# Softmax denominators of a local attention: the reciprocal of a 1x512 row, taken instead as 128x4 after a turn through TensorE

## The chip, the cores and the metric

One Trainium2 chip, all 8 NeuronCores, one launch. Each core works alone on its own half of a sequence (no collectives). The time is that of the slowest core in device microseconds (us). Engines: PE is TensorE (PEld its weight loads), DVE is VectorE, ACT is ScalarE, POOL is GpSimd, SP is SyncE.

## What is computed

Input x of 4 sequences x 8192 tokens x 1024 channels. A linear attention layer with residual and layer norm comes first, then two layers of this kind, and a last layer norm. The part that the change touches is `local_attention`:

```python
WINDOW, HEADS, DIM_HEAD = 512, 8, 64
def local_attention(q, k, v):            # (b, 8, n, 64)
    w = n // WINDOW
    bq = q.reshape(b, h, w, WINDOW, d) * QK_SCALE
    bk, bv = look_around(k), look_around(v)      # a window and the one before it
    sim = einsum('bhwid,bhwjd->bhwij', bq, bk)
    mask = (i < j) | (i > j + WINDOW) | (j == -1)
    attn = softmax(where(mask, -max, sim), axis=-1)
    return einsum('bhwij,bhwjd->bhwid', attn, bv)
def _layer(x, ...):
    h = shift_token(x); q, k, v = split(h @ wqkv)
    q, k = rotary_xpos(l2norm(q) * qs, l2norm(k) * ksc)
    x = x + local_attention(q, k, v) @ wo
    ...                                   # then x + a gated MLP (1024 -> 2 x 2730 -> 1024)
```

## The kernel before

The activations X stay in SBUF, transposed (channels on partitions, 5248 token columns: 4096 of the core and a halo of 1152). The program is a list of operations per engine; `Sched` turns each stated dependency into a wait on a counting semaphore of the engine that does the work, and every engine executes its list strictly in the order in which the Python code adds to it. So the order of the code is the order of the queues.

For each of the two layers, the loop of `build_layer`, `for w in range(n_iter)`, runs over windows of 512 tokens. One pass projects V (`piece_v`), Q and K (`piece_q`, `piece_k`) of window w, turns Q and K to channel-major with float32 transposes on PE into the PSUM bank P[4] (`piece_T`, lines 1049 and 1063), multiplies an earlier window by `wo` (line 1115), and then does the attention of window w-1 for its 8 heads. In the part for one head the keys of that window come in four tiles of 128 (j = 0 to 3). For each tile PE computes scores of up to 640 queries into PSUM (line 1209) and adds the masks as matmuls (lines 1216, 1220), ACT takes the exponential into `pt` (lines 1223, 1227), and PE multiplies by V (`emit_pv`, lines 1164 and 1171). V has a 65th column of ones, so that row 64 of the result is the sum of the exponentials, the denominator of the softmax. Queries of the same window go to bank P[6], those of the next to P[7]; P[7] is carried in `O_acc` until the next window adds its part.

After the fourth tile comes the division, for 80 heads of the first layer and 72 of the second, 152 in all. DVE adds P[6] and `O_acc` into `tsum` (65x512, line 1242); row 64, which lies on one partition, is held above 1e-30 (line 1244), inverted (RECIPROCAL, line 1246) and cast to bf16 as `rrowb` (line 1248). PE spreads it over 64 partitions by a matmul with a column of ones (line 1250, into P[2]), and DVE multiplies (`o_sb`, line 1254). Then DVE copies P[7] to `O_acc` (line 1259); in the last window of a layer, where nothing is carried, a memset stands there. The matmul of line 1250 stands in PE's queue between the last V product of one head and the first scores of the next, so nothing of the next head starts on PE before `rrowb` is there:

```python
trp = s.add("tensor", lambda t: t.matmul(
    P[2][0:64, 0:512], sb["ones_row"][0:1, 0:64], rrowb[0:1, :],
    start=True, stop=True), [tcb, t_tt1, t_uq, t_uk])
```

Behind the two layers stands the last layer norm. Its lines 1650 to 1666 are read below for the price of operations: a RECIPROCAL of a 1x128 row (line 1650), two float32 matmuls that spread a 1x128 row over 128 partitions (lines 1655, 1658), and DVE's use of the first (line 1662).

Of the kernel before, what the change touches and what calls it, by code (L numbers as in the profile page):

```python
# [6 lines left out]
F32 = mybir.dt.float32  # L7
BF16 = mybir.dt.bfloat16
AF = mybir.ActivationFunctionType
ALU = mybir.AluOpType  # L10
# [180 lines left out]
def make_core_inputs(inputs, core):  # L191
    b, h = core // 2, core % 2
    s = 4096 * h
# [94 lines left out]
    for hh in range(8):  # L288
        hs[hh, hh, :] = 1.0
    d["hsel"] = hs  # L290
    d["halo01"] = np.full((128, 1), 1.0 if s > 0 else 0.0, np.float32)
    return d

# [5 lines left out]
class KB:  # L299
# [24 lines left out]
    def build_io(self):  # L324
        d = self.din
# [24 lines left out]
        d("tab", (TEXT, 4, DF))  # L350
        d("ones2row", (2, MEGA))
        d("halo01", (128, 1))
        d("hsel", (8, 8, 128))
        for m in ("mq_lo", "mq_hi", "mk_lo", "mk_hi", "ident", "negI"):
            d(m, (128, 128))
# [14 lines left out]
    def build_consts(self):  # L370
        s, sb, inp = self.s, self.sb, self.inp
        for n, shp, dt in [
            ("ones_row", (1, 640), BF16), ("ones_col", (128, 1), BF16),
            ("identF", (128, 128), F32),
            ("negI", (128, 128), BF16),
            ("mk_lo", (128, 128), BF16), ("mk_hi", (128, 128), BF16),
            ("eps", (128, 1), F32), ("maskrow", (128, NT_EXT), F32),
            ("zrow", (1, 512), BF16),
            ("X", (128, NCH, TEXT), BF16),
            ("lg_col0", (128, NCH), BF16), ("lb_col0", (128, NCH), BF16),  # L380
            ("lg_col1", (128, NCH), BF16), ("lb_col1", (128, NCH), BF16),
            ("b2_col0", (128, NCH), F32), ("b2_col1", (128, NCH), F32),
            ("halo01", (128, 1), F32),
        ]:
            sb[n] = self.sbuf(n + "_g", shp, dt)

        dco = s.new_dma_sem("consts", group=True)
# [3 lines left out]
        s.dma(g, sb["identF"][:, :], inp["ident"][:, :], dco)  # L391
        s.dma(g, sb["maskrow"][:, :], inp["maskrow_col"][:, :], dco)
        s.dma(g, sb["halo01"][:, :], inp["halo01"][:, :], dco)
        for l in range(2):
            s.dma(g, sb[f"lg_col{l}"][:, :], inp[f"lg_col{l}"][:, :], dco)
            s.dma(g, sb[f"lb_col{l}"][:, :], inp[f"lb_col{l}"][:, :], dco)
            s.dma(g, sb[f"b2_col{l}"][:, :], inp[f"b2_col{l}"][:, :], dco)
# [420 lines left out]
    def build_layer(self, l, do_mlp=True):  # L818
# [11 lines left out]
        with ExitStack() as es:  # L830
# [13 lines left out]
            o_sb = [self.sbuf(f"osb{l}_0", (128, 4, 512), BF16, es)]  # L844
            tsum = self.sbuf(f"tsum{l}", (65, 512), F32, es)
            rrowb = self.sbuf(f"rrowb{l}", (1, 512), BF16, es)
            ubuf = self.sbuf(f"ubuf{l}", (128, 512), BF16, es)
            qhat = self.sbuf(f"qhat{l}", (128, 512), BF16, es)
            qrot = self.sbuf(f"qrot{l}", (128, 512), F32, es)
# [51 lines left out]
            self.t_ttk = None  # L901
            self.t_qe_prev = None
            self.t_ke_prev = None
            t_pv = None
            t_oacc = None
            t_tt1 = None
# [172 lines left out]
            for w in range(n_iter):  # L1079
# [61 lines left out]
                if 0 <= pb < n_proj and (do_left or do_right):  # L1141
# [8 lines left out]
                    for h in range(HEADS_F):  # L1150
# [90 lines left out]
                        if do_left:  # L1241
                            tt1 = s.add("vector", lambda v, h=h: v.tensor_add(
                                tsum[:, :], P[6][0:65, :], O_acc[:, h, :]), [t_pv, t_oacc])
                            tmx = s.add("vector", lambda v: v.tensor_scalar(  # L1244
                                tsum[64:65, :], tsum[64:65, :], 1e-30, None, ALU.max), [tt1])
                            trc = s.add("vector", lambda v: v.reciprocal(  # L1246
                                tsum[64:65, :], tsum[64:65, :]), [tmx])
                            tcb = s.add("vector", lambda v: v.tensor_copy(  # L1248
                                rrowb[0:1, :], tsum[64:65, :]), [trc])
                            trp = s.add("tensor", lambda t: t.matmul(  # L1250
                                P[2][0:64, 0:512], sb["ones_row"][0:1, 0:64], rrowb[0:1, :],
                                start=True, stop=True), [tcb, t_tt1, t_uq, t_uk])
                            t_rep = trp
                            to2 = s.add("vector", lambda v, h=h, B=B_left: v.tensor_tensor(
                                o_sb[0][64 * (h % 2):64 * (h % 2) + 64, h // 2, :],
# [472 lines left out]
```

How the kernel before makes its waits and increments, by code:

```python
                def body(eng):  # L101
# [1 line left out]
                    for op in ops[e]:  # L103
                        for d in op.deps:
                            if d.value is None:
                                raise RuntimeError(f"unmarked dep on {e} #{op.idx}")
                            if d.dma_sem is not None:
                                key, sem = d.dma_sem, d.dma_sem.sem
                                val = d.dma_sem.count if d.dma_sem.group else d.value
                            else:
                                key, sem, val = d.engine, sems[d.engine], d.value
                            if val > seen.get(key, 0):
                                eng.wait_ge(sem, val)
                                seen[key] = val
                        inst = op.fn(eng)
                        try:
                            self.inst_map[inst.ins.name] = (e, op.idx, getattr(op, 'label', None))
                        except Exception:
                            pass
                        if op.dma_sem is not None:
                            inst.then_inc(op.dma_sem.sem, 16)
                        elif op.marked:
                            inst.then_inc(sems[e], 1)
                    return None
# [1549 lines left out]
            def fin(sy):  # L1674
                sy.wait_ge(dout[0].sem, dout[0].count)
                sy.wait_ge(dout[1].sem, dout[1].count)
                return None
# [32 lines left out]
            def fin(sy):  # L1710
                sy.wait_ge(dsem.sem, dsem.count)
                return None
```

## Time and profile before

| | |
|---|---|
| median of 2 runs | 11750.34 us (11729.5 to 11771.19) |
| profiled execution, its own time | 11762.71 us |
| its span on the slowest core (core 5) | 11761.1 us |
| spans of the eight cores | 11641.0 to 11761.1 us |
| busy in the span: PE, DVE, ACT | 6636.5 us (56%), 3399.7 us (29%), 1649.8 us (14%) |
| TensorE's granted clock, mean over the span | 0.73 of full speed |

The span runs from the first to the last instruction of a core; the execution's own time is 1.6 us longer. Records of PE overlap, since matmuls are pipelined: the length of one record is not what it costs in a row of them; the distance of two starts is. The bracket behind an instruction is how long its engine had been idle before it, and what ended that.

### The profile page before, as it was taken

Reading aid. Unit: us, or ns where it says so; the run is one execution under the profiler, and the core shown is the slowest. Engines: PE = TensorE matmul, PEld = TensorE weight load, DVE = VectorE, ACT = ScalarE, POOL = GpSimd, SP = SyncE. Lnnn points to the kernel's source line nnn. Section 1 sums busy time; section 2 is a strip of 40 time slices with the busy share of each in tenths; the row PEclk is TensorE's granted clock in tenths of the full one; section 3 lists DMA queues with packets and bytes.
Section 4 is the critical chain, followed back from the end, with each engine's and each line's share of the span. In section 5 each row is a group of like instructions: output and inputs, shape, how many; then the busy total and the mean of one; then the engine's idle time right before and its main releaser. Section 6 shows DMA issues by size and latency. Waiting matters only on the chain.

```text
span 11761.1 us, 75679 instructions; the slowest of 8 cores (11641.0 to 11761.1 us)
## 1 busy us (share of the span) xinstructions
PE 6636.5 (56%) x27498; PEld 2698.4 (23%) x27498; DVE 3399.7 (29%) x4612; ACT 1649.8 (14%) x2817; POOL 91.3 (1%) x136
## 2 busy tenths in 40 slices
PE   0488645544444445447687775544454457778731
PEld 0133212211212222213232222222122123223211
DVE  0011133333443443441112211344434421221234
ACT  0000011111212222210001000222222200000100
POOL 1000000000000000000000000000000000000000
PEclk9977777676666566656799997566666567899965
DMA  9401200001000000001122223000000001222221
GB/s 118 53 0 14 38 0 7 8 7 24 2 1 2 1 1 2 0 8 24 50 67 52 63 69 79 2 2 1 1 2 1 0 17 24 61 63 75 53 60 50
DMA packets 610314, 325.45 MB, mean 28 GB/s; under 512 B 489180, under 2 KB 541004, under 8 KB 608416
## 3 DMA queue, kind: packets, MB, share of 16 engines
q0 software_dynamic: 65024, 79.23, 5.5%
q1 hardware_dynamic: 310496, 137.55, 4.5%
q10 hardware_dynamic: 234432, 103.83, 3.5%
q8 instruction: 228, 3.74, 0.1%
q14 instruction: 134, 1.10, 0.0%
HBM read 374.31 MB, written 59.77 MB: 37 GB/s over the span
## 4 chain that ended last, share of the span: by engine, by line
PE 47%; DVE 26%; DMA 10%; issue 7%; ACT 6%; another core or an unknown queue 4%; DVEq 1%; ACTq 0%; POOL 0%; SPq 0%; POOLq 0%
PE M0b L1519 6%; PE M1b L1519 5%; DVE tsum L1246 4%; DMA w2b<-w2bf 4%; DMA w1g<-w1bf 4%; PE kps L486 3%; PE vps L497 3%; PE M0b L1576 2%; PE p2b L747 2%; PE p2b L653 2%; PE M1b L1576 2%; PE p2b L632 1%; PE L0b L1115 1%; DMA x1t<-x1b 1%
## 5 line engine op out<-in xcount | busy, mean ns | idle before, releaser
L1246 DVE RECIPROCAL tsum<-tsum 1x512 f32<-1x512 f32 x152 | 508.3, 3344 | 16.0 <-DVE tsum L1244 0.5
L1576 PE MATMUL M0b<-hbuf,w2b 128*128 128x512 bf16 (+1 forms) x1760 | 407.2, 385 | 172.0 <-DMA w2b<-w2bf 121.2
L1519 PE MATMUL M0b<-xt,w1a 128*128 128x512 bf16 (+1 forms) x1760 | 448.3, 404 | 89.2 <-DVE xt L1478 69.1
L486 PE MATMUL kps<-WkSb,X_g 128*128 128x512 bf16 x656 | 210.4, 479 | 421.1 <-DMA WvSb<-Wv 421.1
L1519 PE MATMUL M0b<-xt,w1g 128*128 128x512 bf16 (+1 forms) x1760 | 409.9, 378 | 58.6 <-DMA w1g<-w1bf 56.6
L1519 PE MATMUL M1b<-xt,w1a 128*128 128x512 bf16 x1408 | 389.7, 427 | 77.0 <-DVE xt L1478 56.7
L1552 DVE SCALAR_TENSOR_TENSOR hbuf<-M0b,gout 128x512 bf16<-128x512 f32 x220 | 143.4, 652 | 997.2 <-ACT gout L1544 985.7
L1576 PE MATMUL M1b<-hbuf,w2b 128*128 128x512 bf16 x1408 | 338.2, 391 | 131.0 <-DMA w2b<-w2bf 89.9
L1552 DVE SCALAR_TENSOR_TENSOR hbuf<-M1b,gout 128x512 bf16<-128x512 f32 x176 | 121.8, 692 | 840.9 <-ACT gout L1544 831.4
L1519 PE MATMUL M1b<-xt,w1g 128*128 128x512 bf16 x1408 | 343.7, 388 | 26.8 <-DMA w1g<-w1bf 25.3
L1223 ACT ACTIVATE pt<-L0b,mrowH 128x512 bf16<-128x512 f32 (+1 forms) x320 | 213.7, 671 | 681.7 <-PE L0b L1220 583.1
L1223 ACT ACTIVATE pt<-L1b,mrowH 128x512 bf16<-128x512 f32 (+1 forms) x320 | 213.7, 671 | 634.4 <-PE L1b L1220 536.4
L1250 PE MATMUL L0b<-rrowb,ones_row_g 1*64 1x512 bf16 x80 | 48.1, 601 | 440.6 <-DVE rrowb L1248 440.6
L1544 ACT ACTIVATE gout<-M0b 128x512 bf16<-128x512 f32 x220 | 124.4, 565 | 1094.8 <-PE M0b L1535 631.1
L729 PE MATMUL p2tp<-ident_s,gated 128*128 128x128 bf16 x328 | 41.4, 306 | 406.9 <-DVE gated L718 406.9
L1250 PE MATMUL L1b<-rrowb,ones_row_g 1*64 1x512 bf16 x72 | 43.2, 600 | 396.7 <-DVE rrowb L1248 396.7
L1576 PEld LDWEIGHTS M0b<-hbuf,w2b 128*128 128x128 bf16 x1760 | 165.4, 104 | 413.2 <-issue 278.8
L632 PE MATMUL p2b<-X_g,WqSb 128*128 128x512 bf16 (+1 forms) x704 | 176.8, 423 | 141.6 <-DVE X_g L804 87.5
L747 PE MATMUL p2b<-gatedT,WoSb 128*128 128x512 bf16 (+1 forms) x704 | 199.8, 440 | 83.1 <-ACT ao L751 69.3
L512 DVE TENSOR_SCALAR ktile<-ktile,mask_ext_s 128x1024 bf16<-128x1024 bf16 x41 | 20.0, 487 | 756.8 <-ACT ktile L510 756.8
L1544 ACT ACTIVATE gout<-M1b 128x512 bf16<-128x512 f32 x176 | 105.1, 597 | 944.5 <-PE M1b L1535 486.8
L1519 PEld LDWEIGHTS M0b<-xt,w1a 128*128 128x128 bf16 x1760 | 160.6, 104 | 323.0 <-issue 206.7
(358 smaller groups left out, 10560.5 us busy)
## 6 DMA issues: line engine op xcount, KB each, us to landing
w1a<-w1bf SPq DMA_DIRECT2D x198, 256.0 KB, 3.3
w1g<-w1bf ACTq DMA_DIRECT2D x198, 256.0 KB, 3.4
w2b<-w2bf SPq DMA_DIRECT2D x198, 256.0 KB, 2.6
w2b<-w2bf ACTq DMA_DIRECT2D x198, 256.0 KB, 2.6
w1bf<-w POOLq DMA_DIRECT2D x8, 2816.0 KB, 206.8
outT<-fin_o SPq DMA_DIRECT2D x32, 512.0 KB, 3.4
w2bf<-w POOLq DMA_DIRECT2D x8, 1408.0 KB, 276.7
X_g<-x_extT POOLq DMA_DIRECT2D x4, 2624.0 KB, 43.4
```

The source lines that it names most:

```text
L486: mm = s.add("tensor", lambda t, c=c, half=half, xs=xsl, st=(c == 0): t.matmul(kps[half][:, :], xs(c), Wk[:, c, 512 * half:512 * (half + 1 ...
L497: mm = s.add("tensor", lambda t, c=c, half=half, xs=xsl, st=(c == 0): t.matmul(vps[half][:, :], xs(c), Wv[:, c, 512 * half:512 * (half + 1 ...
L632: mm = s.add("tensor", lambda t, c=c, fin=fin, pb=pb, g0=g0, Ng=Ng, st=(fin == 0): t.matmul(P[pb][:, 0:Ng], Wq[:, fin, 128 * c:128 * (c + 1)],
L653: mm = s.add("tensor", lambda t, c=c, half=half, pb=pb, tcol=tcol, st=(c == 0): t.matmul(P[pb][:, :], sb["X"][:, c, tcol:tcol + 128], Wh[: ...
L747: mm = s.add("tensor", lambda t, c=c, fin=fin, pb=pb, Ng=Ng, st=(fin == 0): t.matmul(P[pb][:, 0:Ng], Wo[:, fin, 128 * c:128 * (c + 1)], ga ...
L1115: mm = s.add("tensor", lambda t, c=c, fin=fin, wbank=wbank, B=B, st=(fin == 0): t.matmul(wbank[:, :], wo[:, fin, 128 * c:128 * (c + 1)], o ...
L1223: e1 = s.add("scalar", lambda sc, j=j, kti=kti, qn=qn, bankF=bankF: sc.activation(pt[j % 2][:, 0:min(qn, 512)], bankF[:, 0:min(qn, 512)], ...
L1246: trc = s.add("vector", lambda v: v.reciprocal(tsum[64:65, :], tsum[64:65, :]), [tmx])
L1519: mm = s.add("tensor", lambda t, banks=banks, wt=wt, half=half, fin=fin, nn=nn, st=(fin == 0): t.matmul(banks[half][:, 0:nn], wt[:, fin, : ...
L1544: tg = s.add("scalar", lambda sc, jb=jb, half=half, nn=nn: sc.activation(gout[:, 512 * half:512 * half + nn], P[jb + 2 + half][:, 0:nn], A ...
L1552: th = s.add("vector", lambda v, j=j, jb=jb, half=half, nn=nn: v.scalar_tensor_tensor(h_buf[:, j, 512 * half:512 * half + nn], P[jb + half ...
L1576: mm = s.add("tensor", lambda t, c=c, j=j, sl=sl, half=half, nn=nn, st=(j == 0), sp=(j == 21): t.matmul(P[c][:, 0:nn], w2b[sl][:, 128 * c: ...
```

## The change

Between the addition of line 1242 and the spreading matmul, the three DVE operations on the 1x512 row (maximum, reciprocal, cast) are replaced by a turn of the row onto 128 partitions and back. DVE copies row 64 to `rrowf` on partition 0 (float32). Four float32 matmuls with one row of contraction take 128 of its values each as the stationary operand and a row of `e4` (1x4, a one at place c) as the moving one, and sum up in P[4] as a 128x4 tile. DVE takes the maximum there in place and the reciprocal into `r4sb` (128x4). Four transposes with the float32 identity turn its columns back to 1x128 pieces of row 0 of P[4], and DVE casts this 1x512 row from PSUM to `rrowb`. `e4` is a new input of 1x16 values, loaded on POOL's queue among the constants; `rrowf` and `r4sb` are new SBUF tiles.

```diff
@@ build_consts @@
         s.dma(g, sb["halo01"][:, :], inp["halo01"][:, :], dco)
+        s.dma(g, sb["e4"][:, :], inp["e4"][:, :], dco)
@@ build_layer @@
+            rrowf = self.sbuf(f"rrowf{l}", (1, 512), F32, es)
+            r4sb = self.sbuf(f"r4sb{l}", (128, 4), F32, es)
...
                             tt1 = s.add("vector", lambda v, h=h: v.tensor_add(
                                 tsum[:, :], P[6][0:65, :], O_acc[:, h, :]), [t_pv, t_oacc])
-                            tmx = s.add("vector", lambda v: v.tensor_scalar(
-                                tsum[64:65, :], tsum[64:65, :], 1e-30, None, ALU.max), [tt1])
-                            trc = s.add("vector", lambda v: v.reciprocal(
-                                tsum[64:65, :], tsum[64:65, :]), [tmx])
-                            tcb = s.add("vector", lambda v: v.tensor_copy(
-                                rrowb[0:1, :], tsum[64:65, :]), [trc])
+                            tcp = s.add("vector", lambda v: v.tensor_copy(
+                                rrowf[0:1, :], tsum[64:65, :]), [tt1])
+                            fm = None
+                            for c4 in range(4):
+                                fm = s.add("tensor", lambda t, c4=c4, st=(c4 == 0): t.matmul(
+                                    P[4][:, 0:4],
+                                    rrowf[0:1, 128 * c4:128 * (c4 + 1)],
+                                    sb["e4"][0:1, 4 * c4:4 * c4 + 4],
+                                    start=st, stop=(c4 == 3)),
+                                    [tcp, self.t_cpr, t_tke_last] if c4 == 0 else [])
+                            flr = s.add("vector", lambda v: v.tensor_scalar(
+                                P[4][:, 0:4], P[4][:, 0:4], 1e-30, None, ALU.max), [fm])
+                            rcp = s.add("vector", lambda v: v.reciprocal(
+                                r4sb[:, :], P[4][:, 0:4]), [flr])
+                            bt = None
+                            for c4 in range(4):
+                                bt = s.add("tensor", lambda t, c4=c4: t.transpose(
+                                    P[4][0:1, 128 * c4:128 * (c4 + 1)],
+                                    r4sb[:, c4:c4 + 1], sb["identF"][:, :]),
+                                    [rcp] if c4 == 0 else [])
+                            cpr = s.add("vector", lambda v: v.tensor_copy(
+                                rrowb[0:1, :], P[4][0:1, 0:512]), [bt])
+                            self.t_cpr = cpr
                             trp = s.add("tensor", lambda t: t.matmul(
                                 P[2][0:64, 0:512], sb["ones_row"][0:1, 0:64], rrowb[0:1, :],
-                                start=True, stop=True), [tcb, t_tt1, t_uq, t_uk])
+                                start=True, stop=True), [cpr, t_tt1, t_uq, t_uk])
```

The changed code moves the line numbers behind it: 1242 becomes 1251, 1254 becomes 1280, 1209 becomes 1218, 1171 becomes 1180, and so on.

PE's queue at the end of one head and the start of the next, before (pt and vt in the V product, rrowb in the spreading matmul, qf and kfe in the next head's scores):

```order
L1164 MATMUL L0b<-pt_1,vt_0 65x128 [waits chain_scalar]
L1171 MATMUL L0b<-pt_1,vt_0 65x512
L1250 MATMUL L0b<-rrowb,ones_row_g 64x512 [waits chain_vector]
L1209 MATMUL L0b<-qf_0,kfe_0 128x512
L1209 MATMUL L0b<-qf_1,kfe_0 128x128
```

and the same place in the changed kernel:

```order
L1173 MATMUL L0b<-pt_1,vt_0 65x128 [waits chain_scalar]
L1180 MATMUL L0b<-pt_1,vt_0 65x512
L1257 MATMUL L0b<-e_g,rrowf 128x4 [waits chain_vector]
L1257 MATMUL L0b<-e_g,rrowf 128x4 x3
L1269 MATMUL L0b<-identF_g,r4sb 1x128 [waits chain_vector]
L1269 MATMUL L0b<-identF_g,r4sb 1x128 x3
L1276 MATMUL L0b<-rrowb,ones_row_g 64x512 [waits chain_vector]
L1218 MATMUL L0b<-qf_0,kfe_0 128x512
```

One wait of PE on DVE has become three, with eight small matmuls between them; the next head's scores still stand behind all of it.

DVE's queue for one head, before (tsum is the sum, osb the divided result, Oacc the part that is carried):

```order
L1242 TENSOR_TENSOR tsum<-L0b,Oacc 65x512 [waits chain_tensor]
L1244 TENSOR_SCALAR tsum<-tsum 1x512 [waits chain_vector]
L1246 RECIPROCAL tsum<-tsum 1x512 [waits chain_vector]
L1248 CAST rrowb<-tsum 1x512 [waits chain_vector]
L1254 TENSOR_TENSOR osb_0<-tsum,L0b 64x512 [waits chain_tensor]
L1259 CAST Oacc<-L0b 65x512 [waits chain_vector]
```

and in the changed kernel:

```order
L1251 TENSOR_TENSOR tsum<-L0b,Oacc 65x512 [waits chain_tensor]
L1253 COPY rrowf<-tsum 1x512 [waits chain_vector]
L1263 TENSOR_SCALAR L0b<-L0b 128x4 [waits chain_tensor]
L1265 RECIPROCAL r4sb<-L0b 128x4 [waits chain_vector]
L1273 CAST rrowb<-L0b 1x512 [waits chain_tensor]
L1280 TENSOR_TENSOR osb_0<-tsum,L0b 64x512 [waits chain_tensor]
L1285 CAST Oacc<-L0b 65x512 [waits chain_vector]
```

DVE has one instruction more per head, and waits for PE three times in this stretch where it waited once.

## Rows read from the trace of the kernel before

**Rows 1.** The page: granted clock in 40 slices, and the chain that ended last.
```profile
PEclk9977777676666566656799997566666567899965
...
PE 47%; DVE 26%; DMA 10%; issue 7%; ACT 6%; another core or an unknown queue 4%; DVEq 1%; ACTq 0%; POOL 0%; SPq 0%; POOLq 0%
PE M0b L1519 6%; PE M1b L1519 5%; DVE tsum L1246 4%; DMA w2b<-w2bf 4%; DMA w1g<-w1bf 4%; PE kps L486 3%; PE vps L497 3%; PE M0b L1576 2%; PE p2b L747 2%; PE p2b L653 2%; PE M1b L1576 2%; PE p2b L632 1%; PE L0b L1115 1%; DMA x1t<-x1b 1%
```

**Rows 2.** The page's costliest groups: count, busy us, mean ns, idle before, releaser.
```profile
L1246 DVE RECIPROCAL tsum<-tsum 1x512 f32<-1x512 f32 x152 | 508.3, 3344 | 16.0 <-DVE tsum L1244 0.5
```

**Rows 3.** Timeline, one head's division: start us, us, engine, line, operation, idle before.
```profile
4296.52 0.69 DVE L1242 TENSOR_TENSOR tsum<-L0b,Oacc 65x512 f32<-65x512 f32 x1 [6.45 <-PE L0b L1171]
4297.31 0.42 DVE L1244 TENSOR_SCALAR tsum<-tsum 1x512 f32<-1x512 f32 x1
4297.83 3.34 DVE L1246 RECIPROCAL tsum<-tsum 1x512 f32<-1x512 f32 x1
4301.28 0.42 DVE L1248 CAST rrowb<-tsum 1x512 bf16<-1x512 f32 x1
...
4301.84 0.60 PE L1250 MATMUL L0b<-rrowb,ones_row_g 1*64 1x512 bf16 x1 [5.50 <-DVE rrowb L1248]
...
4302.55 0.68 DVE L1254 TENSOR_TENSOR osb<-tsum,L0b 64x512 bf16<-64x512 f32 x1 [0.85 <-PE L0b L1250]
```

**Rows 4.** Last layer norm, float32 matmuls: durations ns min/median/max of L1655, then its timeline.
```profile
L1655 PE MATMUL F<-frow,onesf_s x64: 416/482/548, 11264.9 to 11754.3; 1*128 1x128 f32 x64
...
11689.50 0.94 DVE L1650 RECIPROCAL frow<-frow 1x128 f32<-1x128 f32 x1 [0.60 <-ACT frow L1648]
...
11690.69 0.76 PE L1655 MATMUL F<-frow,onesf_s 1*128 1x128 f32 x2 [3.33 <-DVE frow L1650]
...
11691.25 0.63 PE L1658 MATMUL F<-frow,onesf_s 1*128 1x128 f32 x2
11691.63 1.22 DVE L1662 TENSOR_TENSOR fin_o<-fin_t,F 128x1024 f32<-128x1024 f32 x1 [0.80 <-PE F L1655]
```

**Rows 5.** Timeline, float32 transposes of Q; then the same place by stretches (columns: Rows 7).
```profile
4162.11 1.09 PE L1049 MATMUL L0b<-identF_g,qrot 128*128 128x128 f32 x4 [7.42 <-DVE qrot L1018]
...
4163.29 0.59 ACT L1053 CAST qf<-L0b 128x512 bf16<-128x512 f32 x1 [5.48 <-PE L0b L1049]
...
4162.00:4164.00 2.00, 1.09 (x4) 0.72 (x4) 1.62 (x4) 0.59 (x1) 0.00 (x0) 0.50 0.04 8
```

**Rows 6.** Groups of DVE instructions from 3100 to 5150 us, shapes apart (as Rows 2).
```profile
L1259 DVE CAST Oacc<-L0b 65x512 bf16<-65x512 f32 x72 | 49.4, 686 | 7.4
...
L1001 DVE RECIPROCAL bnf<-bnf 128x16 f32<-128x16 f32 x33 | 8.4, 253 | 3.8 <-DVE bnf L999 0.5
...
L999 DVE TENSOR_SCALAR bnf<-bnf 128x16 f32<-128x16 f32 x33 | 5.8, 175 | 24.2 <-ACT bnf L997 24.2
```

**Rows 7.** Stretches: us, busy PE, PEld, DVE, ACT, POOL (instructions), granted clock, DMA, GB/s.
```profile
4282.57:4288.60 6.03, 0.71 (x2) 0.26 (x3) 4.87 (x5) 0.00 (x0) 0.00 (x0) 0.67 0.00 0
4288.60:4296.52 7.92, 5.88 (x28) 2.94 (x26) 1.37 (x2) 4.22 (x8) 0.00 (x0) 0.61 0.00 0
...
4294.50:4298.00 3.50, 0.95 (x5) 0.14 (x3) 1.27 (x3) 1.05 (x2) 0.00 (x0) 0.95 0.00 0
4286.00:4294.40 8.40, 5.53 (x26) 2.95 (x27) 3.01 (x4) 3.16 (x6) 0.00 (x0) 0.50 0.00 0
...
11690.00:11691.00 1.00, 0.31 (x1) 0.34 (x2) 0.72 (x2) 0.00 (x0) 0.00 (x0) 0.50 0.00 0
```

**Rows 8.** Timeline, scores and exponentials of the head that begins at 4288.
```profile
4290.22 0.60 PE L1233 MATMUL L0b<-zrow_g,ones_row_g 1*65 1x512 bf16 x1 [0.87 <-DVE Oacc L1259]
...
4290.75 0.71 PE L1209 MATMUL L0b<-qf,kfo 128*128 128x384 bf16 x3
...
4291.77 0.69 ACT L1223 ACTIVATE pt<-L0b,mrowH 128x512 bf16<-128x512 f32 x1 [1.18 <-PE L0b L1220]
...
4294.62 0.69 ACT L1223 ACTIVATE pt<-L0b,mrowH 128x512 bf16<-128x512 f32 x1 [0.42 <-PE L0b L1220]
```

More of the change, by code:

```diff
@@ L290, in make_core_inputs @@
     d["hsel"] = hs
+    e4 = np.zeros((1, 16), np.float32)
+    for c in range(4):
+        e4[0, 4 * c + c] = 1.0
+    d["e4"] = e4
     d["halo01"] = np.full((128, 1), 1.0 if s > 0 else 0.0, np.float32)
@@ L352, in build_io @@
         d("halo01", (128, 1))
+        d("e4", (1, 16))
         d("hsel", (8, 8, 128))
@@ L382, in build_consts @@
             ("b2_col0", (128, NCH), F32), ("b2_col1", (128, NCH), F32),
-            ("halo01", (128, 1), F32),
+            ("halo01", (128, 1), F32), ("e4", (1, 16), F32),
         ]:
@@ L903, in build_layer @@
             self.t_ke_prev = None
+            self.t_cpr = None
             t_pv = None
```

## The prediction

> **What bounds the kernel now.** I read the chain that ended last first [rows 1]. PE holds 47% of it and DVE 26%, and the largest DVE entry is the RECIPROCAL of line 1246 with 4%. Next the costliest groups [rows 2]: that RECIPROCAL ran 152 times at 3344 ns, 508.3 us in all, and 508.3 of 11761 is 4.3%, so practically every one of them lies on the chain. The granted clock in the slices with attention (the ninth to fifteenth of 40, again further on) is about 0.6 [rows 1]; it will matter for the rivals. Then the timeline of one head [rows 3], which says why: it is a strict relay. DVE starts the sum at 4296.52 after 6.45 us of idleness, the maximum 0.79 us later, the reciprocal after 0.52 more, the cast after 3.45, PE's spreading matmul after 0.56, and DVE's product after 0.71. From the sum's start to the product's start that is 6.03 us, and PE was idle for 5.50 of them. PE can do nothing else there, because the next head's scores stand behind the spreading matmul in its queue. The stretches show it too: in the 6.03 us of another head's division PE was busy for 0.71, in the 7.92 us up to the next sum for 5.88 [rows 7]. A head takes 6.03 + 7.92 = 13.95 us, and what is saved or added in its division shows in full, 152 times.
>
> **What goes.** Maximum, reciprocal and cast with their hand-overs: 0.52 + 3.45 + 0.56 = 4.53 us per head. The 0.79 of the sum and the 0.71 from the spreading matmul to the product stay [rows 3].
>
> **What comes**, in the order of the relay.
>
> 1. Copy of the 1x512 row, float32 in SBUF. The maximum on the same row, same type, took 0.42 us, and I take that. DVE's end to PE's start is 0.14 us before a bf16 matmul [rows 3], but before a float32 one it was 0.25 (reciprocal from 11689.50 for 0.94, matmul at 11690.69) [rows 4]. Together 0.67 us.
>
> 2. Four float32 matmuls, 128 stationary columns by 4 moving ones. The last layer norm has the nearest relative: one row of contraction, 128 stationary and 128 moving columns, float32 [rows 4]. The record counts 64 for 32 passes of the loop, so one such matmul is two instructions. The next matmul starts 0.56 us after the first. Within line 1655 both instructions cover 0.76 us; the second lasts 0.416, so it began 0.34 after the first; within line 1658 they cover 0.63, so 0.21. Distances are then 0.34, 0.22 and 0.21. What do they consist of? The stationary operand is 128 wide here and in the change, the moving one 128 here and 4 there. If the load of 128 float32 columns sets the pace, nothing is gained by the short stream; if the stream does, almost all goes. I take the load, since the first distance of 0.34, in which the second load had nothing to hide behind, is the longest. Eight instructions: 0.34 + 6 x 0.215 = 1.63 us from the first start to the last, the last without its stream 0.416 - 0.21 = 0.20, and 0.11 to DVE (PE's end 4302.44 to 4302.55 [rows 3]). That is 1.94 us.
>
> 3. Maximum on 128x4. A TENSOR_SCALAR on 128x16 took 175 ns [rows 6]; 0.17 and a hand-over inside DVE of 0.10 (4297.21 to 4297.31 [rows 3]) make 0.27 us. It reads and writes PSUM, for which I add nothing.
>
> 4. Reciprocal on 128x4. Two RECIPROCALs, 3344 ns for 512 in a row and 253 for 16 [rows 2, 6], give 3091 / 496 = 6.2 ns per element of a partition, so four of them cost 253 - 12 x 6.2 = 178 ns. It writes float32 for PE: 0.18 + 0.25 = 0.43 us. Here is what the change is after: 3.34 us become 0.18.
>
> 5. Four transposes, 128x1 to 1x128, moving operand the 128x128 identity. Four float32 transposes of 128x128 covered 1.09 us and ACT followed 0.09 later [rows 5]. The stationary operand shrinks to one column, the moving one is the same. I take 1.09 + 0.11 = 1.20 us.
>
> 6. Cast of 1x512, now from PSUM. The 65x512 cast from PSUM took 686 ns against 0.42 for 1x512 in SBUF [rows 6, 3]. 0.69 + 0.14 = 0.83 us.
>
> Sum: 0.67 + 1.94 + 0.27 + 0.43 + 1.20 + 0.83 = 5.34 us come and 4.53 go, +0.81 us per head. 152 x 0.81 = +123 us. The relay has more runners, and what the reciprocal gave is spent on them. In the last window of a layer (16 of the 152 heads) the same relay stands with less around it, and the same difference holds.
>
> The rest costs nothing. PE's extra work lies in its own 5.50 us of idleness. P[4] is free: the transposes of Q and K that use it are all before the first head in PE's queue, and its next use is behind the last spreading matmul. The load of `e4` is one more small DMA in POOL's queue in front of the first loads, below 1 us, once.
>
> One rule of the Trainium skill bears on item 2. "TensorE: Matmul & The Clock Gate", section "LDWEIGHTS", says that a weight load is timed by its columns and not by its contraction rows, columns / 1.2 ns, so 107 ns for 128. That the one-row contraction saves nothing is what the layer norm's rows show; the size is not, they show 0.21 to 0.22. By the page's size the four matmuls would be worth, as an estimate, 1.29 us instead of 1.94, and the sum would be +24 us.
>
> **Bounds.** All these PE rows were taken at a granted clock of 0.50, the 1.2 GHz level [rows 5, 7]. In the division the clock is still high at first: over 4294.50 to 4298.00 it was 0.95, over 4286.00 to 4294.40 0.50 [rows 7]. So some of the float32 matmuls, which would start 1.46 us after the sum, may run at 2.4 GHz. The low end is that everything of the division does: distances halve, item 2 is 0.17 + 6 x 0.11 + 0.20 + 0.11 = 1.14, item 5 about 0.76 (three distances of 0.11 and a last record of 0.32, with 0.11), the spreading matmul's 0.71 becomes 0.50. Then -0.80 - 0.44 - 0.21 + 0.81 = -0.64 us per head, -97 us. The high end is that instructions with a 4-column stream don't overlap at all and each takes a whole record of 0.48 [rows 4]: 8 x 0.48 + 0.11 = 3.95 in place of 1.94, +2.82 per head, +429 us. I stay near the middle value, since the rows for it are of the same operation, type and clock.
>
> **Rivals.**
>
> A. The clock rises. PE's longest pause in a head shrinks from 5.50 us to about 1.5 (sum, copy, hand-over). If this holds the clock up where it is now 0.50, scores and V products gain. From [rows 8]: the zero matmul to the next scores 0.53 us (gain about 0.2), those scores to their exponential 1.02 (about 0.4), the wait of 0.42 before the last exponential (all of it), the spreading matmul 0.2; some 1.2 us per head. With the division as summed that is +0.81 - 1.2 = -0.4 us, -60 us in all; if the division runs at the full clock too, -0.64 - 1.0 = -1.6 us, -250 us, the one way past 2% on the fast side. For it: the shorter pauses. Against it: after 4286 the clock stays 0.50 although PE has the spreading matmul, the first scores and the zero matmul to do, and rises only in the dense stretch that follows; the new work is two short bursts. The Trainium skill speaks on both sides: "TensorE: Matmul & The Clock Gate" says in "Loop structure matters more than you think" that bursts with pauses between them go cold and gapless ones stay warm, and in "Part 4: PE-mode transpose" that transposes don't count as busy in the same way. That last is not shown by any row here.
>
> B. The small float32 matmuls are dear, the high end above. Its place is between the copy and the 128x4 maximum. At 2% of the time, 235 us, the division must have grown by 1.55 us; that is item 2 at 2.7 us or more, 0.31 per instruction and up. For it: no row shows a load of 128 float32 columns behind a stream of 4. Against it: loads overlap matmuls in [rows 4]. Time at about 0.40 per instruction: 3.3 us in place of 1.94, +2.2 per head, +330 us, 12,080.
>
> C. The stream set the pace in [rows 4], not the load. Then eight instructions start some 0.11 us apart, item 2 is about 1.2 and the sum near zero: +10 us, 11,760. The other side of my forecast, "not slower", is A, with 11,690 and decided by whether the clock of the first scores is 0.5 or 1.0.
>
> **How the numbers follow.** The profiled execution took 11762.71 us (span 11761.1 and 1.6 around it), with +123 it is 11,886. The median of the runs is 11750.34, 12 us below, so in terms of the median 11,873 us. My forecast holds with a chance of 0.53, and its own range is 11,810 to 11,950. A has 0.18, of which a fifth lies beyond 2%; B 0.15, most of it beyond 2%; C 0.14. A measurement of this kernel can tell about 2% from no change, 11,515 to 11,985. Faster by more than that 0.04; slower by more 0.13; within 0.83. The range of 11,650 to 12,040 leaves out A's far part and B's upper half.
>
> **What would show it.** In the changed kernel's timeline: sum to product about 6.84 us instead of 6.03; from the first 128x4 matmul to the maximum near 1.94, from the first 1x128 transpose to the cast near 1.2, the RECIPROCAL on 128x4 near 0.18 and the cast from PSUM 0.69; DVE's total busy time down by about 152 x 2.7 us, and the whole kernel all the same not faster. The clock between the spreading matmul and the second group of scores should stay 0.5. I am wrong if it is 1.0 there (A), if the eight instructions take 2.7 us or more (B) or 1.2 or less (C), or if the time from product to next sum is no longer 7.92 us.

## The result: 0.6% slower, and the profile after

| | before | after |
|---|---|---|
| median of the runs | 11759.62 us (42 runs) | 11842.02 us (43 runs) |
| ratio after / before | | 1.0062 (95%: 1.0037 to 1.0086) |
| forecast, in terms of its own "before" | | 11,873 us, a ratio of 1.0104 |

The ratio, like every ratio below, is taken from those executions alone in which neither half of the chip ran behind the other at a lower clock, so it is not the quotient of the two medians.

The change costs 0.62%, 73 us of 11760 (44 to 101). The forecast was +123 us. The sign and the mechanism held; the size was too large by 50 us, and that is the difference of two errors with opposite signs.

The page of the changed kernel, its busy times, clock and chain, to be held against [rows 1]:

```profile
PE 6974.2 (59%) x29322; PEld 2978.4 (25%) x29322; DVE 2984.9 (25%) x4764; ACT 1650.0 (14%) x2817; POOL 91.8 (1%) x137
...
PEclk9999777776555555566899987655556566889965
...
PE 50%; DVE 22%; DMA 10%; issue 7%; ACT 6%; another core or an unknown queue 4%; DVEq 1%; ACTq 0%; POOL 0%; SPq 0%; POOLq 0%
PE M1b L1545 6%; PE M0b L1545 5%; DMA w2b<-w2bf 4%; DMA w1g<-w1bf 4%; PE kps L492 3%; PE vps L503 2%; PE M0b L1602 2%; PE M1b L1602 2%; PE p2b L753 2%; PE p2b L659 2%; PE p2b L638 1%; PE L0b L1124 1%; PE L0b L1257 1%; DMA x1t<-x1b 1%
```

DVE's busy time fell by 415 us (from 3399.7), as meant, and the RECIPROCAL of tsum is gone from the chain. PE's rose by 338 us, and the float32 matmuls of line 1257 stand in the chain instead. The share moved from one engine of the relay to another. The heads of the first layer lie in the eleventh to eighteenth slice (their sums run from 3127 to 5133 us before); in the eleventh to seventeenth the clock is 0.5 throughout, where six of the seven had 0.6 before.

One head's division in the changed kernel, its timeline (start us, us, engine, line, operation, idle before), to be held against [rows 3]:

```profile
3500.86 0.69 DVE L1251 TENSOR_TENSOR tsum<-L0b,Oacc 65x512 f32<-65x512 f32 x1 [6.17 <-PE L0b L1180]
3501.65 0.41 DVE L1253 COPY rrowf<-tsum 1x512 f32<-1x512 f32 x1
3502.21 1.83 PE L1257 MATMUL L0b<-e_g,rrowf 1*128 1x4 f32 x8 [1.53 <-DVE rrowf L1253]
3504.15 0.17 DVE L1263 TENSOR_SCALAR L0b<-L0b 128x4 f32<-128x4 f32 x1 [2.09 <-PE L0b L1257]
3504.43 0.18 DVE L1265 RECIPROCAL r4sb<-L0b 128x4 f32<-128x4 f32 x1
3504.76 1.01 PE L1269 MATMUL L0b<-identF_g,r4sb 128*1 128x128 f32 x4 [0.71 <-DVE r4sb L1265]
3505.88 0.68 DVE L1273 CAST rrowb<-L0b 1x512 bf16<-1x512 f32 x1 [1.26 <-PE L0b L1269]
3506.70 0.60 PE L1276 MATMUL L0b<-rrowb,ones_row_g 1*64 1x512 bf16 x1 [0.93 <-DVE rrowb L1273]
...
3507.41 0.68 DVE L1280 TENSOR_TENSOR osb<-tsum,L0b 64x512 bf16<-64x512 f32 x1 [0.86 <-PE L0b L1276]
```

The reciprocal takes 0.18 us instead of 3.34, and yet the division takes 6.55 us from sum to product instead of 6.03. The largest single piece is now 1.94 us, from the first 128x4 matmul to the maximum.

To weigh all heads and not one, I took the start of every sum and every product from the timelines of both kernels (152 heads each). A head then has two parts: the division, from sum to product, and the rest, from product to the next sum. "Full heads" are those that are followed by another head of their window and carry something to the next (119 of them).

| mean us per head | before | after | difference |
|---|---|---|---|
| division, all 152 | 6.04 | 6.40 | +0.355 |
| rest, 119 full heads | 7.87 | 8.04 | +0.164 |

152 x 0.355 is 54 us, and 0.164 for each of the 136 heads that carry something to the next window is 22 us: 76 us, against 73 measured. The spans of the two profiled executions (11761.1 and 11739.5 us) don't show this, because before the first head ever ran they differ by 109 us (first sum at 3126.76 us on core 5 before, at 3017.60 on core 4 after), with the same instructions and a granted clock in the slices before it that was lower in the first. Stretches of the same work must be compared, not these spans: from the first sum to the last of a layer it is 2005.8 and 1764.8 us before, 2046.2 and 1805.5 after, 81 us more in the two layers. That is for the slowest core of each; as a mean of all eight cores these stretches are 3770 us before and 3840 after, 70 us more.

### The profile page after: what moved, and what is told of

Read it like the earlier page. It is cut to its first block, busy times and chain, and to the rows that moved or that the text cites. A ratio compares the mean times of both kernels' runs of the same rounds, so it can differ in the third digit from the quotient of the medians.

```text
span 11739.5 us, 79936 instructions; the slowest of 8 cores (11703.0 to 11739.5 us)
## 1 busy us (share of the span) xinstructions
PE 6974.2 (59%) x29322; PEld 2978.4 (25%) x29322; DVE 2984.9 (25%) x4764; ACT 1650.0 (14%) x2817; POOL 91.8 (1%) x137
## 4 chain that ended last, share of the span: by engine, by line
PE 50%; DVE 22%; DMA 10%; issue 7%; ACT 6%; another core or an unknown queue 4%; DVEq 1%; ACTq 0%; POOL 0%; SPq 0%; POOLq 0%
PE M1b L1545 6%; PE M0b L1545 5%; DMA w2b<-w2bf 4%; DMA w1g<-w1bf 4%; PE kps L492 3%; PE vps L503 2%; PE M0b L1602 2%; PE M1b L1602 2%; PE p2b L753 2%; PE p2b L659 2%; PE p2b L638 1%; PE L0b L1124 1%; PE L0b L1257 1%; DMA x1t<-x1b 1%
## 5 line engine op out<-in xcount | busy, mean ns | idle before, releaser
L492 PE MATMUL kps<-WkSb,X_g 128*128 128x512 bf16 x656 | 180.9, 425 | 419.6 <-DMA WvSb<-Wv 419.6
L1545 PEld LDWEIGHTS M0b<-xt,w1g 128*128 128x128 bf16 x1760 | 155.4, 101 | 283.2 <-issue 153.1
L1602 PEld LDWEIGHTS M1b<-hbuf,w2b 128*128 128x128 bf16 x1408 | 132.2, 100 | 339.9 <-issue 220.9
L1659 PE MATMUL F<-fin_tb,ones_col_g 128*1 128x128 bf16 x256 | 32.4, 306 | 302.3 <-DVE fin_tb L1653 302.3
L1257 PE MATMUL L0b<-e_g,rrowf 1*128 1x4 f32 x640 | 135.2, 330 | 122.5 <-DVE rrowf L1253 122.5
```

The costliest lines, as they stand in the source:

```text
L492: mm = s.add("tensor", lambda t, c=c, half=half, xs=xsl, st=(c == 0): t.matmul(kps[half][:, :], xs(c), Wk[:, c, 512 * half:512 * (half + 1 ...
L1257: fm = s.add("tensor", lambda t, c4=c4, st=(c4 == 0): t.matmul(P[4][:, 0:4], rrowf[0:1, 128 * c4:128 * (c4 + 1)], sb["e4"][0:1, 4 * c4:4 * ...
L1545: mm = s.add("tensor", lambda t, banks=banks, wt=wt, half=half, fin=fin, nn=nn, st=(fin == 0): t.matmul(banks[half][:, 0:nn], wt[:, fin, : ...
L1602: mm = s.add("tensor", lambda t, c=c, j=j, sl=sl, half=half, nn=nn, st=(j == 0), sp=(j == 21): t.matmul(P[c][:, 0:nn], w2b[sl][:, 128 * c: ...
```

## The experiments

The theory after the result: the division is a relay, each link of it costs its own duration and a hand-over, and the eight float32 matmul instructions with their weight loads are the longest link; the rest of a head grew because the stretches of high clock moved. Rivals: the reciprocal had been partly hidden; the short stream and not the load sets the price; PE's new bursts, and not the length of the pause, cost the 0.16 us outside. All ratios are to runs of the kernel before on the same chip. Each profile is of one execution, and four of the kernels (without the reciprocal, turn in bf16, way back without a copy, division out of PE's way) were timed four times each, so their intervals are wide.

### The reciprocal left out

```diff
-                            trc = s.add("vector", lambda v: v.reciprocal(
-                                tsum[64:65, :], tsum[64:65, :]), [tmx])
+                            trc = tmx
```

> The kernel before without its RECIPROCAL: rows are multiplied by the denominator instead of its inverse (this part is left out); everything else stands. Theory of the relay (every reciprocal lies in full on the chain): the division falls from 6.04 to about 2.6 us per head, 152 x 3.45 = 524 us less, -4.5%. Rival (the reciprocal is partly covered, by ACT or by a later wait): well under 400 us less. Beside that the stretch from product to next sum may move by +-0.2 us per head with the granted clock.

The relay of one head without it:

```profile
3066.13 0.42 DVE L1244 TENSOR_SCALAR tsum<-tsum 1x512 f32<-1x512 f32 x1
3066.65 0.42 DVE L1247 CAST rrowb<-tsum 1x512 bf16<-1x512 f32 x1
```

Measured: ratio 0.9537 (0.9482 to 0.9591), -4.6%; the division 2.52 us on average, the rest 7.87. 152 x (6.04 - 2.52) = 535 us are 4.6% of 11730. Nothing of the reciprocal was hidden. The change aimed at the right place, and up to 535 us were to be had there.

### Sixteen times as many moving columns

```diff
-                                    P[4][:, 0:4],
+                                    P[4][:, 0:64],
                                     rrowf[0:1, 128 * c4:128 * (c4 + 1)],
-                                    sb["e4"][0:1, 4 * c4:4 * c4 + 4],
+                                    sb["e4"][0:1, 64 * c4:64 * c4 + 64],
```

The input `e4` is widened from 16 to 256 values to match.

> The changed kernel with 64 instead of 4 moving columns in the four float32 matmuls (60 of them zero). If the load of the 128 float32 columns sets their pace (0.21 to 0.22 us per instruction), the time from the first of them to the 128x4 maximum stays at 1.94 us or grows by 0.1 at most (the last stream), and the kernel stays within 20 us of the changed one, 0.6% above before. If load and stream add up, eight streams of 64 float32 columns (about 0.1 us each at 1.2 GHz, half of the 0.21 for 128) bring +0.8 us per head, +120 us, 1.6% above before.

The timeline of its first turn, with its first two instructions by themselves on the second line:

```profile
3505.00 1.93 PE L1257 MATMUL L0b<-e_g,rrowf 1*128 1x64 f32 x8 [1.53 <-DVE rrowf L1253]
...
3505.00 0.65 PE L1257 MATMUL L0b<-e_g,rrowf 1*128 1x64 f32 x2 [1.53 <-DVE rrowf L1253]
...
3507.04 0.17 DVE L1263 TENSOR_SCALAR L0b<-L0b 128x4 f32<-128x4 f32 x1 [2.19 <-PE L0b L1257]
```

The same two instructions in the changed kernel, and the lengths of all its records there (ns, min/median/max):

```profile
3502.21 0.55 PE L1257 MATMUL L0b<-e_g,rrowf 1*128 1x4 f32 x2 [1.53 <-DVE rrowf L1253]
...
L1257 PE MATMUL L0b<-e_g,rrowf x640: 239/349/351, 3018.9 to 5066.6; 1*128 1x4 f32 x160
```

First matmul to maximum 2.04 us, against 1.94 with 4 columns: 0.10 more. Of that 0.07 is the longer last record (0.416 us, not 0.349), and 0.03 the first distance, from the first start to the second: by the single records 0.237 us, not 0.205 (the lines above give 0.65 - 0.416 and 0.55 - 0.349). The six distances behind it are 0.213 us in both kernels: there a stream sixteen times as long costs nothing. The ratio, 1.0095 (1.0061 to 1.0129), is 0.33%, 39 us, above that of the changed kernel, where I had allowed 20, but the two intervals overlap, and the 1.6% of loads and streams added up is outside; the stretches from first to last sum grew by 12 us (2051.3 and 1812.5). The stream doesn't set the pace; rival C of the prediction falls.

That it is the load which sets the pace is not shown by this. The float32 transposes of line 1269, with one stationary column and 128 moving ones, start 0.213 us apart as well (median of 456 distances at a clock of 0.50 on core 4; the first of each three is 0.17). Either a load of 128 columns and a stream of 128 happen to cost the same, or every float32 instruction costs 0.213 us there. No run has both short.

### The first turn in bf16

```diff
-            rrowf = self.sbuf(f"rrowf{l}", (1, 512), F32, es)
+            rrowf = self.sbuf(f"rrowf{l}", (1, 512), BF16, es)
...
-            ("halo01", (128, 1), F32), ("e4", (1, 16), F32),
+            ("halo01", (128, 1), F32), ("e4", (1, 16), BF16),
```

> The changed kernel with the first turn in bf16: rrowf and e4 are bf16, so the four matmuls are four instructions with 128-column bf16 loads instead of eight float32 ones. Theory (the price is the float32 loads): from the first of them to the 128x4 maximum 0.7 to 0.8 us instead of 1.94, the division 5.2 us instead of 6.40, 120 to 140 us less than before, -1.1%. Rival (each instruction costs 0.21 whatever its type): 1.0 us, division 5.45, about 90 us less than before.

Its timeline, from the copy to the maximum:

```profile
3496.28 0.41 DVE L1253 CAST rrowf<-tsum 1x512 bf16<-1x512 f32 x1
3496.81 0.18 PEld L1257 LDWEIGHTS L0b<-e_g,rrowf 1*128 1x128 bf16 x4 [2.05 <-issue]
3496.84 0.24 PE L1257 MATMUL L0b<-e_g,rrowf 1*128 1x4 bf16 x4 [1.53 <-DVE rrowf L1253]
3497.19 0.17 DVE L1263 TENSOR_SCALAR L0b<-L0b 128x4 f32<-128x4 f32 x1 [0.49 <-PE L0b L1257]
```

The busy times and the granted clock of this kernel over the same matmuls (the columns are those of [rows 7]):

```profile
3496.80:3497.20 0.40, 0.24 (x4) 0.18 (x4) 0.01 (x1) 0.00 (x0) 0.00 (x0) 0.50 0.00 0
```

Ratio 0.9795 (0.9705 to 0.9885): faster than before, by 1.15 to 2.95%, from one change of type; the profile accounts for the low end, 144 us or 1.2% from first to last sum (1918.9 and 1707.8 us). First matmul to maximum 0.35 us instead of 1.94; the division fell to 4.96 us, below both expectations. The four bf16 matmuls cover 0.24 us at a clock of 0.50 with records of 0.161, so they start (0.24 - 0.161) / 3 = 0.026 us apart, each with a load of 128 columns. The eight float32 ones start 0.21 apart on average ((1.83 - 0.349) / 7). It is not the instruction count alone that costs: halved in number, the price fell to less than a fifth. It is the type: a float32 instruction with a load of 128 columns. And the rest of a head did not come back with the shorter division: it is 8.07 us, longer than before.

### The way back without a copy

As above, and:

```diff
+                                with self.nc.allow_low_precision(reason="bf16 denominators"):
+                                    return v.reciprocal(r4sb[:, :], P[4][:, 0:4])
...
-                                bt = s.add("tensor", lambda t, c4=c4: t.transpose(
-                                    P[4][0:1, 128 * c4:128 * (c4 + 1)],
-                                    r4sb[:, c4:c4 + 1], sb["identF"][:, :]),
...
-                            cpr = s.add("vector", lambda v: v.tensor_copy(
-                                rrowb[0:1, :], P[4][0:1, 0:512]), [bt])
...
+                                trp = s.add("tensor", lambda t, c4=c4: t.matmul(
+                                    P[2][0:64, 128 * c4:128 * (c4 + 1)],
+                                    bass.AP(r4sb, c4, [[4, 128], [0, 64]]),
+                                    sb["identB"][:, :], start=True, stop=True),
```

> As the kernel with the turn in bf16, and the way back cut: the reciprocal is written as bf16, and four bf16 matmuls with a column of it, repeated 64 times, as stationary and the identity as moving operand write the spread row straight into P[2]; the transposes, the cast from PSUM and the spreading matmul go. Relay: 0.79 + 0.56 + 0.75 + 0.28 + 0.33 + 0.75 = 3.5 us instead of 6.04 before, -2.5 x 152 = -390 us, -3.3%. Rival (shorter pauses change the clock): if the clock stays high the rest falls too, down to -4.5%.

Its timeline, from reciprocal to product:

```profile
3501.18 0.18 DVE L1268 RECIPROCAL r4sb<-L0b 128x4 bf16<-128x4 f32 x1
...
3501.51 0.61 PE L1272 MATMUL L0b<-identB_g,r4sb 128*64 128x128 bf16 x4 [0.71 <-DVE r4sb L1268]
3502.22 0.68 DVE L1279 TENSOR_TENSOR osb<-tsum,L0b 64x512 bf16<-64x512 f32 x1 [0.86 <-PE L0b L1272]
```

Ratio 0.9548 (0.9459 to 0.9636). The column of denominators, r4sb, is bf16 here, and each matmul spreads it over 64 rows by a stride of zero. Reciprocal to product is 1.04 us, against 2.98 in the changed kernel (3504.43 to 3507.41); the division is 3.03 us, the rest 8.04. I had expected 3.5 us and -3.3%. The time hit the number of the rival, -4.5%, but not its mechanism: the rest did not fall, it is 8.04 us against 7.87 before. From the first to the last sum the profile shows 427 us less than before (1775.0 and 1568.9), 3.6%, the low end of an interval that rests on few executions. The idea of the change is sound with two links fewer and bf16 in the ones that stay.

### A longer pause with nothing new on PE

```diff
+            padrow = self.sbuf(f"padrow{l}", (1, 512), F32, es)
...
+                            tpad = s.add("vector", lambda v: v.tensor_copy(
+                                padrow[0:1, :], tsum[64:65, :]), [tt1])
                             tmx = s.add("vector", lambda v: v.tensor_scalar(
-                                tsum[64:65, :], tsum[64:65, :], 1e-30, None, ALU.max), [tt1])
+                                tsum[64:65, :], tsum[64:65, :], 1e-30, None, ALU.max), [tpad])
```

> The kernel before with one more 1x512 float32 copy on DVE between sum and maximum, and nothing new on PE. It asks where the 0.16 us per head come from that the changed kernel lost outside the division. The division must grow by 0.52 to 0.55 us, 80 to 84 us in all. Theory clock (a longer pause moves the stretches of high clock away from the V products): the rest of a head grows too, from 7.87 to about 8.0 us, and the kernel by about 100 us, +0.9%. Rival (PE's new bursts or the use of bank P[4] cost it): the rest stays at 7.87, +0.7%.

Measured: ratio 1.0070 (1.0035 to 1.0106), which fits both expectations (+0.9% and +0.7%); the parts of a head decide. The division is 6.56 us (+0.52), and the rest 8.03 instead of 7.87, although neither PE's queue nor the work of the rest was touched. I then took the granted clock of the last 1 us before each sum, where the last V product runs, in every full head:

| full heads | clock above 0.9 there | below 0.6 | their rest, us |
|---|---|---|---|
| before | 110 | 9 | 7.84 / 8.24 |
| after | 72 | 47 | 7.90 / 8.25 |
| with the extra copy | 66 | 53 | 7.88 / 8.21 |

In the changed kernel a head whose last V product runs at the high level is 0.35 us shorter. It has 38 more of the slow kind among 119, 38 / 119 x 0.35 = 0.11 us, and most of the remaining 0.05 is in the fast kind (7.90 against 7.84), where the clock rises 1.81 us before the sum on average and rose 1.97 before it in the kernel before. The row of that product shows it too (count, busy us, mean ns). In the kernel before:

```profile
L1171 PE MATMUL L0b<-pt,vt 128*65 128x512 bf16 x72 | 28.4, 395 | 0.0
```

In the changed kernel:

```profile
L1180 PE MATMUL L0b<-pt,vt 128*65 128x512 bf16 x72 | 35.1, 487 | 0.0
```

With the extra copy:

```profile
L1172 PE MATMUL L0b<-pt,vt 128*65 128x512 bf16 x72 | 34.8, 483 | 0.0
```

The same in single heads (the columns are those of [rows 7]). In the kernel before, the last 1 us ahead of the sum at 4296.52, at the high level:

```profile
4295.52:4296.52 1.00, 0.43 (x2) 0.14 (x2) 0.00 (x0) 0.25 (x1) 0.00 (x0) 1.00 0.00 0
```

With the extra copy, the last 1 us ahead of the sum at 3327.16, at the low level:

```profile
3326.16:3327.16 1.00, 0.71 (x2) 0.19 (x2) 0.00 (x0) 0.00 (x0) 0.00 (x0) 0.50 0.00 0
```

So the 0.16 us go with the clock, and PE's new bursts are not needed for them: the extra copy on DVE alone gives the same. What decides where the stretches of high clock fall stays open. It is not simply that the pause is longer. Over all eight cores the slow kind is this many of 119 heads on average, beside the division and the rest in us:

| | division | slow heads | rest |
|---|---|---|---|
| no reciprocal | 2.53 | 14 | 7.89 |
| way back without a copy | 3.03 | 51 | 8.03 |
| turn in bf16 | 4.96 | 69 | 8.08 |
| before | 6.04 | 14 | 7.88 |
| changed kernel | 6.39 | 48 | 8.04 |
| extra copy | 6.56 | 54 | 8.03 |

Two kernels with a shorter division than before, both with the bursts, have the long rest too, and the shortest of all, without them, has not. That bursts add something in those two is not excluded; no run has such a length without them.

### PE's pause filled

```diff
                         if do_left:
+                            for dm in range(12):
+                                s.add("tensor", lambda t, dm=dm: t.matmul(
+                                    P[4][:, :], wo[:, 0, 0:128], wo[:, 1, 0:512],
+                                    start=True, stop=True),
+                                    [t_tke_last, t_w] if dm == 0 else [])
                             tt1 = s.add("vector", lambda v, h=h: v.tensor_add(
```

> The kernel before with twelve 128x512 bf16 matmuls on the weights into the unused bank P[4] in PE's pause of each head; nothing reads them. At 1.2 GHz they take 12 x 0.43 = 5.1 us, within the pause of 5.5. It prices the clock. Theory clock: granted clock near 1.0 in scores and V products, the rest of a head falls from 7.87 to 6.7 to 7.1 us, the spreading matmul by 0.2; 130 to 200 us less, -1.1 to -1.7%. Rival (the rest is set by ACT and the hand-overs, not by PE's clock): the clock rises and the time stays within 40 us of before.

Stretches of one head: division, scores of the first two key tiles, the others (the columns are those of [rows 7]):

```profile
3504.15:3509.95 5.80, 4.40 (x13) 1.54 (x13) 4.87 (x4) 0.00 (x0) 0.00 (x0) 0.75 0.00 0
3509.95:3513.50 3.55, 1.91 (x17) 1.11 (x15) 1.37 (x2) 1.93 (x4) 0.00 (x0) 1.00 0.00 0
3513.50:3517.56 4.06, 2.88 (x12) 1.51 (x13) 0.00 (x0) 2.18 (x5) 0.00 (x0) 0.54 0.01 4
```

Ratio 0.9936 (0.9909 to 0.9964). Neither expectation held. The clock did come up, and the division fell by 0.17 us (the spreading matmul). But in this head it went down again in the middle of the scores, whose matmuls at the full clock left PE idle for almost half of the second stretch (1.91 of 3.55 us), and the third ran at 0.54. Over all full heads the rest is 7.82 us against 7.87 (7.81 to 7.85 on the eight cores), while I had forecast 6.7 to 7.1. The high clock was moved from the end of the head to its start, where part of it is hidden behind DVE's copy to O_acc: PE waits 1.24 us for that copy there, and 0.87 where the clock is low [rows 8]:

```profile
3511.57 0.37 PE L1233 MATMUL L0b<-zrow_g,ones_row_g 1*65 1x512 bf16 x1 [1.24 <-DVE Oacc L1264]
```

Filling this one pause, by twelve matmuls, did not hold it. So the price that rival A of the prediction put on a clock that is high throughout was not tested either. From first to last sum this profile accounts for 29 us of the gain, and 40 as a mean of all eight cores; where the remainder of the measured 0.64% (75 us, 42 to 107) lies, I did not find.

### The division taken out of PE's way

The kernel before, reciprocal and all, with the order of the queues changed: the copy to O_acc comes right after the sum, and the spreading matmul and the product of a head are emitted behind the scores of the next one's key tile 3 (the window's last head right after its loop). The core of it:

```diff
+                    def flush():
...
+                        trp = s.add("tensor", lambda t: t.matmul(
+                            P[2][0:64, 0:512], sb["ones_row"][0:1, 0:64], rrowb[0:1, :],
+                            start=True, stop=True), [tcb_, t_tt1, t_uq, t_uk])
...
+                        t_tt1 = s.add("vector", lambda v, h=hp, B=B_left: v.tensor_tensor(
...
+                        flush()
                         t_pv = emit_pv(*pend)
...
+                            defer = (h, tcb)
+                    flush()
```

> The kernel before with its reciprocal as it was, but the spreading matmul and the product of a head are put behind the scores of the next head, and the copy to O_acc before the maximum; the last head of a window is divided at once. Theory (the cost of the reciprocal is its place in PE's queue): a full head takes 8.0 to 8.8 us instead of 13.92, 7 of 8 heads gain, 133 x 5.1 to 5.9 = 680 to 790 us less, -5.8 to -6.7%. Rival (DVE becomes the bound): DVE has 6.2 us of work and 0.6 of hand-overs per head and would not bind below 7; if it does through its waits for PE, a head takes 10 us or more and the gain is under 520 us.

Its timeline over one head:

```profile
3571.14 0.69 DVE L1260 TENSOR_TENSOR tsum<-L0b,Oacc 65x512 f32<-65x512 f32 x1 [7.57 <-PE L0b L1188]
...
3571.93 0.69 DVE L1264 CAST Oacc<-L0b 65x512 bf16<-65x512 f32 x1
...
3573.16 3.34 DVE L1273 RECIPROCAL tsum<-tsum 1x512 f32<-1x512 f32 x1
3573.30 0.71 PE L1226 MATMUL L0b<-qf,kfo 128*128 128x384 bf16 x3
...
3577.54 0.63 PE L1159 MATMUL L0b<-rrowb,ones_row_g 1*64 1x512 bf16 x1
...
3578.27 0.68 DVE L1163 TENSOR_TENSOR osb<-tsum,L0b 64x512 bf16<-64x512 f32 x1 [1.25 <-PE L0b L1159]
...
3579.35 0.69 DVE L1260 TENSOR_TENSOR tsum<-L0b,Oacc 65x512 f32<-65x512 f32 x1 [0.40 <-PE L0b L1188]
```

Ratio 0.9316 (0.9242 to 0.9389), the fastest of all, 6.8% below before, 719 to 891 us. The reciprocal still takes 3.34 us, but PE computes scores beside it, and a full head takes 7.92 us on average instead of 13.92. Over all 133 heads that have another behind them in their window, those of the last windows with less work included, it is 7.87 instead of 13.52: 133 x 5.65 = 751 us, and 743 from first to last sum, within that interval. The copy to O_acc comes earlier here as well; its part in the gain was not separated. In the 8.21 us of the head shown PE is busy for 6.82 and DVE for 6.22, with waits of 1.25 us before the product and 0.40 before the next sum (the columns are those of [rows 7]):

```profile
3571.14:3579.35 8.21, 6.82 (x30) 3.36 (x29) 6.22 (x6) 4.22 (x8) 0.00 (x0) 0.50 0.00 0
```

## Why the forecast was right, and what it had wrong

- The view was right: every link of the division is on the path. The kernel without the reciprocal gained all of it and a little more (535 us, 524 expected).
- The sum's direction was right: the new links cost more than the 4.53 us that went. At a clock of 0.50, item by item, the forecast against the changed kernel's timeline: copy and hand-over 0.67, measured 0.56; float32 matmuls 1.94, measured 1.94; maximum 0.27, measured 0.28; reciprocal and hand-over 0.43, measured 0.33; transposes 1.20, measured 1.12; cast 0.83, measured 0.82. The choice that decided the sign, that the price does not go with the stream, was right, and the experiment with 64 columns confirms it.
- That item 2 came out at 1.94 to the hundredth is luck. It was summed as 1.63 us from the first start to the last and 0.31 from there to the maximum; measured are 1.48 and 0.46. The first distance was taken as 0.34 and is 0.205, and the last record doesn't shrink to 0.20 but lasts 0.349. Nor does the reason given for the load hold ("the first distance of 0.34, in which the second load had nothing to hide behind, is the longest"). With a load of 128 columns every time, the first distance is 0.205, 0.237 and 0.343 us for 4, 64 and 128 moving columns: it grows with the stream, and in the changed kernel it is the shortest of the seven. What stays the same with 4 and with 64 columns is the later distances, 0.213.
- The step that was off is "DVE's end to PE's start before a float32 matmul is 0.25 us". I took it from the layer norm [rows 4] and charged it twice; in the changed kernel it is 0.15 both times, as before a bf16 matmul. There it is 0.25 in 28 of 32 passes, so the reading was right and only its transfer failed; why it is longer there was not tried. The other mis-sized term is the transposes, 1.12 and not 1.20. Together these are 0.29 us: 6.55 instead of 6.84.
- "I stay near the middle value" took the clock as 0.50 throughout the division. The low bound had the rest of it: in some heads the clock is still high when the float32 matmuls run, and the shortest division took 5.73 us. The mean of all 152 is 6.40, another 0.15 lower than the head shown. Division in all: +0.355 us, not +0.81.
- The step "what stands outside the division stays at 7.92 us" failed, and I had named it only as a sign of being wrong. The rest grew by 0.16 us per head (8.04 against 7.87), with the clock, in the direction opposite to rival A. So -69 us on the first error (152 x 0.455) and +22 on the second, which makes 123 into 76.
- Rival A (the clock rises) didn't come about. The clock from product to three microseconds before the next sum was 0.50 on average in both kernels. No run shows what a clock that is high throughout would bring. Rival B (small float32 matmuls at full record length) and C (the stream) are excluded by 1.94 us and by the 64 columns.
- Where the Trainium skill, "TensorE: Matmul & The Clock Gate", section "LDWEIGHTS", gives columns / 1.2 ns for a load, 107 ns for 128 columns, the pace of neither type follows it here: float32 instructions stood 0.21 us apart, bf16 ones 0.026, at the same clock, though one bf16 load record by itself lasts 0.10 us. The estimate of 1.29 us for item 2 by that rule missed the 1.94. Its section "Weight-path perf modes — Fast Weight Load (FWL) and DoubleRow" says that a load of 128 non-float32 weights takes a faster path and float32 doesn't, and the two types agree with it in direction.
- One reading of the rows was wrong without a consequence: the attention is not in the ninth to fifteenth slice but in the eleventh to eighteenth; the clock there is 0.5 to 0.6 before.

## What to carry to other kernels

Before an operation on the path is made cheaper by a detour, count the links of the detour: each turn through PE and back cost 0.26 us in hand-overs alone (0.15 and 0.11) besides its work, and a float32 matmul with 128 stationary columns cost 0.21 us per instruction at a clock of 0.50, two instructions to a matmul. Ask first whether the next piece of work has to stand behind the slow operation in the queue at all: with the end of the division moved behind the next head's scores, the same 3.34 us reciprocal ran beside PE's work, and that was worth 6.8% where the best detour brought 4.5%. If the detour stays, keep it in bf16 and let its last matmul write what the consumer reads.

## What the runs showed of the hardware

- A float32 matmul with 128 stationary columns and 4 moving ones is two instructions with loads, 1.83 us for four of them at a clock of 0.50; in bf16 the same four took 0.24 us. From the first to the maximum that is 0.35 us instead of 1.94, where I had expected 0.7 to 0.8.
- RECIPROCAL on DVE goes by the elements of a partition: 512 on one partition took 3344 ns, 16 on each of 128 took 253, 4 on each of 128 took 183.
- Half a microsecond more of DVE work per head moved the clock's high stretches so that 53 of 119 last V products ran at the low level instead of 9, and cost another 0.15 us per head outside the division. A small change in the length of a cycle can change its other parts without touching them.
